# Attention of a two-layer kernel: the value products cut into two halves of 256 queries, in slots 1 and 3, and the key projection moved from slot 1 to slot 2

## The chip, the cores and the metric

The kernel runs on one core of one Trainium2 chip. The metric is the device time of one execution in microseconds, the median of several runs. Engines are named as in the profile: PE (TensorE, matrix products), PEld (its weight loads, which overlap PE), DVE (VectorE), ACT (ScalarE), POOL (GpSimd) and SP (SyncE, which issues most transfers).

## What is computed

Two layers act on `x` (8 batches of 512 tokens, 256 wide) and a context of the same shape. The first has a gated linear attention (mLSTM) and an MLP; the second has a softmax attention with 16 heads of 64 and a mixture of eight experts. All data is f32. The change touches only the softmax attention:

```python
q = query @ W_Query + B_Query          # W_*: 256 x 1024
k = key @ W_Key + B_Key                # key = value = the context
v = value @ W_Value + B_Value
q = q.reshape(B, Lq, H, D)             # H = 16, D = 64
k = k.reshape(B, Lk, H, D)
v = v.reshape(B, Lk, H, D)
scores = jnp.einsum('bqhd,bkhd->bhqk', q, k) / D ** 0.5
probs = jax.nn.softmax(scores, axis=-1)
out = jnp.einsum('bhqk,bkhd->bqhd', probs, v).reshape(B, Lq, H * D)
return out @ W_Output + B_Output
```

## The kernel before

`attention` works through U = 64 units `u`: 8 batches times 8 pairs of heads. The two heads of a pair fill the 128 partitions (64 each). A unit has NBL = 8 blocks `j`: head `j // 4`, 128 queries each. Each engine runs a program written out by hand, and all of them walk through the same loop: for every unit, eight slots `j` from 0 to 7. The text calls the score product of block j S(j) and the turn (the transposing product) of block j T(j).

The steps of a block are:

- S(j), in slot j, on PE (`score`, L917): two products of 128x512 in fp32r, into one of two banks of PSUM (`j % 2`). S(j) waits until the exponential of block j-2 has read that bank.
- the row maximum on DVE (L1052), the exponential with its row sum on ACT (L1009), the reciprocal of the sum on DVE (L1057), the scaling of the 128x512 block on POOL (L1030).
- T(j) on PE (`turn`, L928): four transposes of 128x128, in slot j+2 (T(6) and T(7) fall into slots 0 and 1 of the next unit). It waits for POOL.
- the copy of the turned block into `PT` on DVE (`keep`, L1064), for j = 4 and 5 on ACT (L1022).

Around these blocks PE does the rest of the unit's neighbours. `project` (L896, four passes of 512 columns) makes the queries of unit u+1 in slot 0 and its keys in slot 1. `weigh_values` (L938) makes the value products of unit u-1 in slot 2. `project_values` (L905) makes the values of u+1 in slot 4, and `output` (L948) the output products of u-1 in slots 5 and 6:

```python
if j < 2 and there(u + 1):
    project(u + 1, j)
if j == 2 and there(u - 1):
    weigh_values(u - 1)
```

In `weigh_values`, each head's V is the stationary operand with 64 columns. Head 0 goes to the left half of the array (PSUM partitions 0 to 63) and head 1 to the right half, so the products of the two heads run side by side. All other products of this loop use the array as 128 x 128. One product of f32 stands in the trace as two instructions: the eight products of `weigh_values` are 16 records. The first waits for all eight turned copies of the unit, for V, and for the output additions of the unit before (`x`); the last raises `pv`. On ACT `heads_out` (L995) then copies bank O_BANK to `oT`, before the exponential of slot 4, and `output` reads `oT`. ACT's `keys` (L985, in slot 1) and DVE's `keys` (L1046, in slot 2) write the two parts of `k_own`, and SP then copies them into `k2` with four transfers (L879), which S(0) of the next unit waits for. `add_out` (L1071) on DVE adds the output products to x in slot 7.

Of the kernel before, what the change touches and what calls it, by code (L numbers as in the profile page):

```python
# [21 lines left out]
P = 128  # L22
B, S, D = 8, 512, 256
N = B * S
TPB = S // P
# [5 lines left out]
AH, AD = 16, 64  # L31
# [794 lines left out]
def attention(nc, c, x_all, xnT_all, ctxT_all, first, Wq, Wk, Wv, Wo):  # L826
# [3 lines left out]
    with ExitStack() as ctx:  # L830
# [36 lines left out]
        with nc.Block() as block:  # L867
# [15 lines left out]
            def _(pe):  # L883
# [47 lines left out]

                def weigh_values(u):
                    wait_turned_copies(pe, u, NBL)
                    pe.wait_ge(s["V"], u + 1)
                    wait_count(pe, s["x"], 2 * u)
                    for t in range(TPB):
                        for h in range(2):
                            ins = pe.matmul(ps[AD * h:AD * h + AD, O_BANK, :], V[:, u % 2, t, AD * h:AD * h + AD],  # L938
                                            PT[:, u % 2, h, t, :], start=t == 0, stop=t == TPB - 1)
                    ins.then_inc(s["pv"], 1)  # L940

# [13 lines left out]
                for u in range(U + 1):  # L955
                    for j in range(NBL):
# [4 lines left out]
                        if j < 2 and there(u - 1):  # L961
                            turn(u - 1, NBL - 2 + j)
                        if j < 2 and there(u + 1):
                            project(u + 1, j)
                        if j == 2 and there(u - 1):
                            weigh_values(u - 1)
                        if j == 4 and there(u + 1):
# [5 lines left out]
            def _(act):  # L973
# [28 lines left out]
                for u in range(U + 1):  # L1002
                    for j in range(NBL):
                        if j == 4 and there(u - 1):
                            heads_out(u - 1)
                        if there(u):
                            act.wait_ge(s["nmax"], NBL * u + j + 1)
                            wait_count(act, s["t_ps"], NBL * u + j - 3)
                            act.activation(Pr[:, j % 4, :], ps[:, S_BANK + j % 2, :], ACT.Exp,  # L1009
                                           bias=nmax[:, j % 4:j % 4 + 1], accum_out=rsum[:, j % 4:j % 4 + 1]  # L1010
                                           ).then_inc(s["exp"], 1)
                        if there(u + 1):
                            if j == 0:
                                queries(u + 1)
                            if j == 1:
                                keys(u + 1)
# [17 lines left out]
            def _(dve):  # L1034
# [48 lines left out]
                for u in range(U + 1):  # L1083
                    for j in range(NBL):
# [8 lines left out]
                        if there(u + 1):  # L1093
                            if j == 1:
                                queries(u + 1)
                            if j == 2:
                                keys(u + 1)
# [635 lines left out]
```

## Time and profile before

| | before |
|---|---|
| median of 3 runs | 1862.72 us (1861.0 to 1865.55) |
| the profiled execution, own time | 1861.19 us |
| its span | 1859.5 us |
| PE busy in the span | 1683.3 us (91%) |
| DVE, ACT, POOL busy | 1192.0, 842.8, 619.9 us |
| mean granted clock of TensorE | 0.943 of full speed |

The span is the stretch from the first to the last record of the profiled execution; its own time is 1.7 us longer. An engine's busy time counts the stretches in which at least one of its instructions stands in the records. The ends of PE's records are modelled, so distances between starts say more about PE than the durations do. The attention lies roughly between 460 and 1640 us.

### The profile page before, as it was taken

The numbers are of one execution on the slowest core, as the hardware profiler recorded it, in microseconds if no ns is written. First come the engines' busy times: TensorE is split into PE (matmuls) and PEld (weight loads), VectorE is DVE, ScalarE is ACT, GpSimd is POOL, SyncE is SP. The second block draws the span as 40 slices with busy tenths as digits, with TensorE's granted clock in tenths as the row PEclk, the third lists the DMA queues.
The fourth block names the chain that finished last, engine by engine and source line by source line (L and its number), as shares of the span: only waits on it lengthen the run. The fifth ranks groups of instructions, "written<-read, shape, count | busy, mean of one in ns | idle before, by whom it ended". The sixth has DMA issues, their size and how long they took to land. (4 is left out here: it accounts for less than half of the span.)

```text
span 1859.5 us, 26060 instructions
## 1 busy us (share of the span) xinstructions
PE 1683.3 (91%) x8890; PEld 1152.6 (62%) x8890; DVE 1192.0 (64%) x2642; ACT 842.8 (45%) x1870; POOL 619.9 (33%) x746
## 2 busy tenths in 40 slices
PE   6469999996999999999999999999999999873584
PEld 4357777764666666666666666666666666572352
DVE  6444454432777777777777777777777777667761
ACT  3324443431555555555555555555555555421110
POOL 2154444430333232333333233232323232210375
PEclk9669999997999999999999999999999999955797
DMA  7100000003323222232323223232322223144144
GB/s 258 21 22 13 12 12 1 1 0 105 69 46 69 53 61 64 51 69 46 69 48 67 56 58 68 46 69 46 68 51 64 58 57 69 23 146 132 44 85 57
DMA packets 66657, 109.46 MB, mean 59 GB/s; under 512 B 16088, under 2 KB 48096, under 8 KB 66528
## 3 DMA queue, kind: packets, MB, share of 16 engines
q1 hardware_dynamic: 60384, 99.29, 21.8%
q0 software_dynamic: 6144, 8.52, 2.8%
q8 instruction: 72, 1.18, 0.3%
q14 instruction: 57, 0.47, 0.1%
HBM read 27.84 MB, written 12.85 MB: 22 GB/s over the span
## 5 line engine op out<-in xcount | busy, mean ns | idle before, releaser
L1030 POOL TENSOR_SCALAR at_Pr<-at_Pr,at_rinv 128x512 f32<-128x512 f32 x512 | 354.1, 692 | 826.7 <-DVE at_rinv L1057 826.7
L1009 ACT ACTIVATE at_Pr<-at_ps,at_nmax 128x512 f32<-128x512 f32 x512 | 352.0, 687 | 522.7 <-DVE at_nmax L1052 521.1
L1052 DVE TENSOR_REDUCE at_nmax<-at_ps 128x1 f32<-128x512 f32 x512 | 350.9, 685 | 139.0 <-PE at_ps L917 128.0
L917 PE MATMUL at_ps<-at_k,at_q 128*128 128x512 f32 x1024 | 420.8, 492 | 9.7 <-DMA at_k<-at_k_own 8.0
L928 PE MATMUL at_ps<-k_ident,at_Pr 128*128 128x128 f32 x2048 | 310.5, 274 | 4.0 <-POOL at_Pr L1030 4.0
L928 PEld LDWEIGHTS at_ps<-k_ident,at_Pr 128*128 128x128 f32 x2048 | 249.5, 140 | 93.2 <-POOL at_Pr L1030 32.8
L1064 DVE COPY at_PT<-at_ps 128x512 f32<-128x512 f32 x384 | 261.3, 681 | 0.0
L917 PEld LDWEIGHTS at_ps<-at_k,at_q 128*128 128x128 f32 x1024 | 174.6, 191 | 129.6 <-issue 120.1
L938 PE MATMUL at_ps<-at_PT,at_V 128*64 128x512 f32 x1024 | 233.8, 598 | 0.9 <-DVE at_PT L1064 0.9
L1057 DVE RECIPROCAL at_rinv<-at_rsum 128x1 f32<-128x1 f32 x512 | 83.3, 163 | 174.5 <-ACT at_Pr L1009 172.5
L938 PEld LDWEIGHTS at_ps<-at_PT,at_V 128*64 128x64 f32 x1024 | 67.7, 136 | 121.5 <-issue 120.3
L948 PE MATMUL at_ps<-at_wo,at_oT 128*128 128x256 f32 x512 | 131.6, 380 | 0.8 <-ACT at_oT L995 0.8
L458 PE MATMUL mm_ps<-mx_w,mm_hT 128*128 128x256 f32 x512 | 120.2, 381 | 0.0
L448 PE MATMUL mm_ps<-m_xnT,mx_w 128*128 128x512 f32 x256 | 111.2, 592 | 1.3 <-ACT m_xnT L601 1.3
L905 PE MATMUL at_ps<-at_w_rest,m_ctxT 128*128 128x128 f32 x896 | 109.2, 275 | 0.0
L896 PE MATMUL at_ps<-m_xnT,at_w_rest 128*128 128x512 f32 x224 | 107.1, 601 | 0.0
L896 PE MATMUL at_ps<-m_ctxT,at_w_rest 128*128 128x512 f32 x224 | 105.5, 593 | 0.0
L905 PEld LDWEIGHTS at_ps<-at_w_rest,m_ctxT 128*128 128x128 f32 x896 | 104.5, 192 | 0.0
L458 PEld LDWEIGHTS mm_ps<-mx_w,mm_hT 128*128 128x128 f32 x512 | 94.2, 190 | 15.5 <-issue 3.8
L1039 DVE SCALAR_TENSOR_TENSOR at_q<-at_ps,m_b_all,at_q 64x512 fp32r<-64x512 f32 x128 | 96.0, 750 | 8.4 <-ACT at_q L978 5.4
L1009 ACT ACTIVATION_READ_ACCUMULATOR at_Pr<-at_ps,at_nmax 128x1 f32 x512 | 98.7, 193 | 0.0
L948 PEld LDWEIGHTS at_ps<-at_wo,at_oT 128*128 128x128 f32 x512 | 87.4, 190 | 8.3 <-ACT at_oT L995 1.7
(237 smaller groups left out, 2030.5 us busy)
## 6 DMA issues: line engine op xcount, KB each, us to landing
at_k<-at_k_own SPq DMA_DIRECT2D x256, 256.0 KB, 4.1
k_x<-in_x SPq DMA_DIRECT2D x8, 512.0 KB, 7.8
mg_ctx<-in_ctx SPq DMA_DIRECT2D x8, 512.0 KB, 8.0
mx_ctxn<-in_ctx SPq DMA_DIRECT2D x8, 512.0 KB, 3.9
rows<-lo_xn SPq DMA_DIRECT2D x8, 512.0 KB, 3.0
out<-k_x SPq DMA_DIRECT2D x1, 4096.0 KB, 14.6
r_w<-in_L_ffn_w SPq DMA_DIRECT2D x16, 256.0 KB, 5.6
mx_w<-in_L_ffn_w SPq DMA_DIRECT2D x2, 1024.0 KB, 9.8
```

What stands on the lines that cost most here:

```text
L448: ins = pe.matmul(ps[:, H_BANK + f % 4, :], w1_s[:, k, P * f:P * f + P], xnT_all[:, k, b * S:b * S + S], start=k == 0, stop=k == DC - 1)
L458: ins = pe.matmul(ps[:, Y_BANK + t // 2, D * (t % 2):D * (t % 2) + D], hT[:, f, P * t:P * t + P], w2_s[:, f, :], start=f == 0, stop=f == F ...
L896: ins = pe.matmul(ps[:, A_BANK + k, :], weights(k, d, hp), src[:, d, b * S:b * S + S], start=d == 0, stop=d == DC - 1)
L905: ins = pe.matmul(ps[:, A_BANK, P * t:P * t + P], ctxT_all[:, d, b * S + P * t:b * S + P * t + P], weights(2, d, hp), start=d == 0, stop=d ...
L917: ins = pe.matmul(ps[:, S_BANK + j % 2, :], q2[:, u % 2, h, q:q + P], k2[:, u % 2, h, part, :], start=part == 0, stop=part == 1)
L928: ins = pe.transpose(ps[:, T_BANK + j % 2, P * t:P * t + P], Pr[:, j % 4, P * t:P * t + P], c["ident"][:, :])
L938: ins = pe.matmul(ps[AD * h:AD * h + AD, O_BANK, :], V[:, u % 2, t, AD * h:AD * h + AD], PT[:, u % 2, h, t, :], start=t == 0, stop=t == TP ...
L948: ins = pe.matmul(ps[:, Y_BANK - half, D * (t % 2):D * (t % 2) + D], oT[:, P * t:P * t + P], wo_s[:, u % HP, :], start=True, stop=True)
L1009: act.activation(Pr[:, j % 4, :], ps[:, S_BANK + j % 2, :], ACT.Exp, bias=nmax[:, j % 4:j % 4 + 1], accum_out=rsum[:, j % 4:j % 4 + 1]).th ...
L1030: pool.tensor_scalar(Pr[:, n % 4, :], Pr[:, n % 4, :], rinv[:, n % 4:n % 4 + 1], 1.0, ALU.mult, ALU.mult).then_inc(s["pn"], 1)
L1052: dve.tensor_reduce(nmax[:, j % 4:j % 4 + 1], ps[:, S_BANK + j % 2, :], AX.X, ALU.max, negate=True).then_inc(s["nmax"], 1)
L1064: dve.tensor_copy(PT[:, u % 2, j // TPB, :, q:q + P], ps[:, T_BANK + j % 2, :].rearrange("p (t q) -> p t q", t=TPB)).then_inc(s["pt_v"], 1)
```

## The change

`weigh_values` takes a half: the first makes queries 0 to 255 of both heads, in slot 1, the second queries 256 to 511, in slot 3. The weights V are the same for both. Within `PT` a block j of either head covers queries `128 * (j % 4)` onwards; the first half waits for the copies of blocks 0 to 5 and the second for all eight. `pv` is raised after the second. The key projection of the next unit moves from slot 1 to slot 2, and ACT's `keys` from slot 1 to slot 2 and DVE's from slot 2 to slot 3 with it. On ACT, `heads_out` goes behind the exponential of slot 4.

```diff
--- before.py
+++ after.py
@@ -929,15 +929,20 @@
                                            c["ident"][:, :])
                     ins.then_inc(s["t_ps"], 1)
 
-                def weigh_values(u):
-                    wait_turned_copies(pe, u, NBL)
-                    pe.wait_ge(s["V"], u + 1)
-                    wait_count(pe, s["x"], 2 * u)
+                def weigh_values(u, half):
+                    if half == 0:
+                        wait_turned_copies(pe, u, NBL - 2)
+                        pe.wait_ge(s["V"], u + 1)
+                        wait_count(pe, s["x"], 2 * u)
+                    else:
+                        wait_turned_copies(pe, u, NBL)
+                    at = slice(2 * P * half, 2 * P * half + 2 * P)
                     for t in range(TPB):
                         for h in range(2):
-                            ins = pe.matmul(ps[AD * h:AD * h + AD, O_BANK, :], V[:, u % 2, t, AD * h:AD * h + AD],
-                                            PT[:, u % 2, h, t, :], start=t == 0, stop=t == TPB - 1)
-                    ins.then_inc(s["pv"], 1)
+                            ins = pe.matmul(ps[AD * h:AD * h + AD, O_BANK, at], V[:, u % 2, t, AD * h:AD * h + AD],
+                                            PT[:, u % 2, h, t, at], start=t == 0, stop=t == TPB - 1)
+                    if half:
+                        ins.then_inc(s["pv"], 1)
 
                 def output(u, half):
                     if half == 0:
@@ -960,10 +965,10 @@
                                 turn(u, j - 2)
                         if j < 2 and there(u - 1):
                             turn(u - 1, NBL - 2 + j)
-                        if j < 2 and there(u + 1):
-                            project(u + 1, j)
-                        if j == 2 and there(u - 1):
-                            weigh_values(u - 1)
+                        if j in (0, 2) and there(u + 1):
+                            project(u + 1, j // 2)
+                        if j in (1, 3) and there(u - 1):
+                            weigh_values(u - 1, j // 2)
                         if j == 4 and there(u + 1):
                             project_values(u + 1)
                         if j in (5, 6) and there(u - 1):
@@ -1001,18 +1006,18 @@
                 values(0)
                 for u in range(U + 1):
                     for j in range(NBL):
-                        if j == 4 and there(u - 1):
-                            heads_out(u - 1)
                         if there(u):
                             act.wait_ge(s["nmax"], NBL * u + j + 1)
                             wait_count(act, s["t_ps"], NBL * u + j - 3)
                             act.activation(Pr[:, j % 4, :], ps[:, S_BANK + j % 2, :], ACT.Exp,
                                            bias=nmax[:, j % 4:j % 4 + 1], accum_out=rsum[:, j % 4:j % 4 + 1]
                                            ).then_inc(s["exp"], 1)
+                        if j == 4 and there(u - 1):
+                            heads_out(u - 1)
                         if there(u + 1):
                             if j == 0:
                                 queries(u + 1)
-                            if j == 1:
+                            if j == 2:
                                 keys(u + 1)
                             if j == 5:
                                 values(u + 1)
@@ -1093,7 +1098,7 @@
                         if there(u + 1):
                             if j == 1:
                                 queries(u + 1)
-                            if j == 2:
+                            if j == 3:
                                 keys(u + 1)
                         if j == 7:
                             if there(u):
```

On PE, from the score product of slot 1 to the projection of the values in slot 4, the program of before has (L917 is a score product, L928 a turn, L896 the key projection, L938 the value products, L905 the projection of the values; one row for what stands together):

```order
L917 MATMUL at_ps<-at_k,at_q 128x512 x2
L928 MATMUL at_ps<-k_ident,at_Pr 128x128 x4
L896 MATMUL at_ps<-m_ctxT,at_w_rest 128x512 x2
L917 MATMUL at_ps<-at_k,at_q 128x512 x2
L928 MATMUL at_ps<-k_ident,at_Pr 128x128 x4
L938 MATMUL at_ps<-at_PT,at_V 64x512 x8
L917 MATMUL at_ps<-at_k,at_q 128x512 x2
L928 MATMUL at_ps<-k_ident,at_Pr 128x128 x4
L917 MATMUL at_ps<-at_k,at_q 128x512 x2
L928 MATMUL at_ps<-k_ident,at_Pr 128x128 x4
L905 MATMUL at_ps<-at_w_rest,m_ctxT 128x128 x8
```

And the changed program over the same slots (L942 are the value products now):

```order
L917 MATMUL at_ps<-at_k,at_q 128x512 x2
L928 MATMUL at_ps<-k_ident,at_Pr 128x128 x4
L942 MATMUL at_ps<-at_PT,at_V 64x256 x8
L917 MATMUL at_ps<-at_k,at_q 128x512 x2
L928 MATMUL at_ps<-k_ident,at_Pr 128x128 x4
L896 MATMUL at_ps<-m_ctxT,at_w_rest 128x512 x2
L917 MATMUL at_ps<-at_k,at_q 128x512 x2
L928 MATMUL at_ps<-k_ident,at_Pr 128x128 x4
L942 MATMUL at_ps<-at_PT,at_V 64x256 x8
L917 MATMUL at_ps<-at_k,at_q 128x512 x2
L928 MATMUL at_ps<-k_ident,at_Pr 128x128 x4
L905 MATMUL at_ps<-at_w_rest,m_ctxT 128x128 x8
```

The one group of eight value products with 512 columns became two groups of eight with 256 columns, each between a turn and a score product, and the key projection stands between the groups.

On ACT, from the exponential of slot 1 on (L1009 exponentials, L985 keys, L995 `heads_out`, L990 values, L1022 a turned copy), before:

```order
L1009 ACTIVATE at_Pr,at_rsum<-at_ps,at_nmax 128x512
L985 ACTIVATE at_k_own<-at_ps,m_b_all 128x512
L1009 ACTIVATE at_Pr,at_rsum<-at_ps,at_nmax 128x512 x2
L995 ACTIVATE at_oT<-at_ps,m_b_all 128x512
L1009 ACTIVATE at_Pr,at_rsum<-at_ps,at_nmax 128x512 x2
L990 COPY at_V<-at_ps 128x512
```

and in the changed program (the same operations are L1012, L990, L1000, L995 and L1027):

```order
L1012 ACTIVATE at_Pr,at_rsum<-at_ps,at_nmax 128x512 x2
L990 ACTIVATE at_k_own<-at_ps,m_b_all 128x512
L1012 ACTIVATE at_Pr,at_rsum<-at_ps,at_nmax 128x512 x2
L1000 ACTIVATE at_oT<-at_ps,m_b_all 128x512
L1012 ACTIVATE at_Pr,at_rsum<-at_ps,at_nmax 128x512
L995 COPY at_V<-at_ps 128x512
```

The keys went one exponential later, and `heads_out` too.

## Rows read from the trace of the kernel before

**Rows 1.** The page: busy time of each engine over the whole span.
```profile
PE 1683.3 (91%) x8890; PEld 1152.6 (62%) x8890; DVE 1192.0 (64%) x2642; ACT 842.8 (45%) x1870; POOL 619.9 (33%) x746
```

**Rows 2.** Busy time by stretch; columns in the first row; steady part of the attention.
```profile
core 0: us, PE busy (x) PEld busy (x) DVE busy (x) ACT busy (x) POOL busy (x), PEclk, DMA share, GB/s
...
1000.00:1300.00 300.00, 300.00 (x1582) 197.55 (x1582) 221.69 (x447) 167.01 (x382) 91.45 (x133) 1.00 0.26 57
```

**Rows 3.** Timeline of PE, one unit: start us, us, engine, line, operation, tiles, count.
```profile
1007.87 0.60 PE L928 MATMUL at_ps<-k_ident,at_Pr 128*128 128x128 f32 x4
1008.40 3.65 PE L938 MATMUL at_ps<-at_PT,at_V 128*64 128x512 f32 x16
1011.98 0.74 PE L917 MATMUL at_ps<-at_k,at_q 128*128 128x512 f32 x2
1012.56 0.60 PE L928 MATMUL at_ps<-k_ident,at_Pr 128*128 128x128 f32 x4
1012.91 0.71 PE L917 MATMUL at_ps<-at_k,at_q 128*128 128x512 f32 x2
1013.47 0.60 PE L928 MATMUL at_ps<-k_ident,at_Pr 128*128 128x128 f32 x4
...
1016.15 0.60 PE L928 MATMUL at_ps<-k_ident,at_Pr 128*128 128x128 f32 x4
1016.59 1.03 PE L948 MATMUL at_ps<-at_wo,at_oT 128*128 128x256 f32 x4
...
1017.92 0.60 PE L928 MATMUL at_ps<-k_ident,at_Pr 128*128 128x128 f32 x4
...
1019.70 0.60 PE L928 MATMUL at_ps<-k_ident,at_Pr 128*128 128x128 f32 x4
...
1020.73 0.66 PE L928 MATMUL at_ps<-k_ident,at_Pr 128*128 128x128 f32 x4
1021.23 1.88 PE L896 MATMUL at_ps<-m_xnT,m_w_first 128*128 128x512 f32 x4
...
1023.41 0.60 PE L928 MATMUL at_ps<-k_ident,at_Pr 128*128 128x128 f32 x4
1023.85 1.88 PE L896 MATMUL at_ps<-m_ctxT,m_w_first 128*128 128x512 f32 x4
...
1026.03 0.60 PE L928 MATMUL at_ps<-k_ident,at_Pr 128*128 128x128 f32 x4
```

**Rows 4.** Timeline of the weight loads (PEld); in brackets, idle time before.
```profile
1008.40 0.20 PEld L938 LDWEIGHTS at_ps<-at_PT,at_V 128*64 128x64 f32 x4 [0.17 <-issue]
1008.88 0.14 PEld L938 LDWEIGHTS at_ps<-at_PT,at_V 128*64 128x64 f32 x2 [0.29 <-issue]
...
1011.03 0.14 PEld L938 LDWEIGHTS at_ps<-at_PT,at_V 128*64 128x64 f32 x2 [0.28 <-issue]
1011.98 0.30 PEld L917 LDWEIGHTS at_ps<-at_k,at_q 128*128 128x128 f32 x2 [0.81 <-issue]
...
1020.73 0.42 PEld L928 LDWEIGHTS at_ps<-k_ident,at_Pr 128*128 128x128 f32 x4 [0.40 <-POOL at_Pr L1030]
```

**Rows 5.** Timeline of the other engines and of SP's queue, same unit.
```profile
1007.92 0.19 ACT L1009 ACTIVATION_READ_ACCUMULATOR at_Pr<-at_ps,at_nmax 128x1 f32 x1
...
1011.22 3.75 SPq L879 DMA_DIRECT2D at_k<-at_k_own  x4
...
1012.76 0.69 DVE L1052 TENSOR_REDUCE at_nmax<-at_ps 128x1 f32<-128x512 f32 x1 [1.55 <-PE at_ps L917]
...
1014.16 0.68 ACT L995 ACTIVATE at_oT<-at_ps,m_b_all 128x512 f32<-128x512 f32 x1
...
1019.99 0.69 POOL L1030 TENSOR_SCALAR at_Pr<-at_Pr,at_rinv 128x512 f32<-128x512 f32 x1 [1.08 <-DVE at_rinv L1057]
```

**Rows 6.** Costliest groups, shapes apart: count, busy us, mean ns of one.
```profile
L948 PE MATMUL at_ps<-at_wo,at_oT 128*128 128x256 f32 x512 | 131.6, 380 | 0.8 <-ACT at_oT L995 0.8
```

## Prediction

> **What bounds the kernel now.** I read the busy times first. PE stands at 91% of the span and the next engine at 64% [rows 1]. In the steady part of the attention PE is busy for all of 300 us, at a granted clock of 1.00 (the 2.4 GHz level), while DVE has 222 us and the others less [rows 2]. But the ends of PE's records are modelled, so "100% busy" could hide waits. So I went to the timeline of PE and measured the distances between the starts of turns; one stands in each slot [rows 3]. The reader is to see that almost every distance is what the products in it need:
>
> - T(1) to T(2), with nothing but a score product between: 1013.47 - 1012.56 = 0.91 us.
> - T(7) to T(0), with the key projection between: 1026.03 - 1023.41 = 2.62 us.
> - T(0) to T(1), with the value products between: 1012.56 - 1007.87 = 4.69 us.
> - T(5) to T(6): 1020.73 - 1019.70 = 1.03 us, 0.12 more than the 0.91 above.
>
> The length of one 512-column pass comes from the weight loads: from 1008.88 to 1011.03 are five passes of a pair of heads, 2.15 / 5 = 0.43 us [rows 4]. The four passes of a projection are then 1.72 us, and 2.62 - 1.72 = 0.90 us is left for a score product and a turn: the same as the 0.91 of the slot that has nothing else. So the slots with a projection hold no wait at all. The unit repeats every 1026.03 - 1007.87 = 18.16 us, and 64 of these are 1162 us, most of the stretch of the attention.
>
> Two things in the unit are not PE's own work. One is the 0.12 us at T(6), which waits for POOL: its scaling ends at 1020.68 [rows 5] and the weight load starts at 1020.73, after 0.40 us of idle time that mostly lies beside the score product [rows 4]. The other is in the value products. Their eight pairs are 8 x 0.43 = 3.44 us, a score and a turn 0.90, together 4.34, and the distance is 4.69: **0.35 us more**. The weight loads show where it lies. At the entrance, the first load stands 0.17 us after the turn's loads, and the next pair's load at 1008.88 puts the start of the first pair at 1008.45, 0.15 us after the end of T(0)'s pass work (1007.87 + 0.43 = 1008.30). At the exit, the load for S(3) comes at 1011.98 after 0.81 us without a load, where 0.28 or 0.29 is the rule [rows 4]; that is the other 0.20. Nothing that S(3) waits for is open then: the exponential that frees its bank had ended at 1008.11 [rows 5]. The row maximum of the same block sat idle for 1.55 us waiting for PE [rows 5], so the other engines follow PE here and not the reverse.
>
> The page "TensorEngine Tiling (Array Packing)" of the Trainium skill, section on tiling modes, says that a change of tiling mode drains the engine. The value products are the only ones of the loop in the form 128*64, and the trace agrees as to place: both parts of the 0.35 us stand exactly where the form changes.
>
> **The change, part by part.**
>
> 1. *A second block of value products.* The form of the products now changes four times in a unit and not twice: turn to value products to score product, in slot 1 and again in slot 3. What one such visit costs the row above gives, 0.35 us. The bounds for the new one: nothing, if the excess goes by the columns and not by the visit; and the whole 0.35. A first pair and a last pair exist in each half as they do in the whole, so I take the upper end: +0.35 us per unit.
>
> 2. *256 columns instead of 512.* A unit has 16 pairs of passes of 256 columns for 8 of 512. The nearest rows are the output products, 256 columns with full weights: four records last 1.03 us and one 0.380 [rows 3, 6], so they follow each other by (1.03 - 0.38) / 3 = 0.217 us. The 16 pairs are 3.47 us for 3.44: +0.03 us. V is loaded twice as often. A pair's loads take 0.14 us [rows 4], less than 0.217, so they stay covered by the pair ahead; without that cover each would add up to 0.14 (a rival, below).
>
> 3. *The key projection in slot 2.* The same four passes, 1.72 us, between T(0) and T(1) now. On PE it costs nothing either way.
>
> 4. *What the moved steps may make late.* ACT's and DVE's parts of the keys come one slot later; the four transfers start about 2 us later in the unit. They took 3.75 us from 1011.22 on [rows 5] and are needed at S(0), which stands between T(5) at 1019.70 and T(6) at 1020.73: some 5 us were spare, 3 remain. `heads_out` now waits for the exponential of S(4). Before, it ended at 1014.16 + 0.68 = 1014.84, that is 2.86 us after the start of the score product that followed the value products (1011.98) [rows 3, 5]. After the change that product is S(4), with the exponential of that block again ahead of `heads_out`. The output products start 1016.59 - 1012.91 = 3.68 us after S(4) [rows 3], so `oT` is there 0.8 us early. Priced at nothing; the cover is the projection of the values between them.
>
> 5. *The wait of T(6).* Slots 4 to 7 keep their order on all engines but for `heads_out`, and the chain from S(6) to T(6) is the same. I leave its 0.12 us as it is, so the more even filling of the early slots wins nothing: there was no wait in them.
>
> **The sum.** From T(7) to T(2), before: 2.62 + 4.69 + 0.91 = 8.22 us. After: 0.90 + 8 x 0.217 + 0.35 = 2.99 for each half, and 2.62 for the keys: 8.60 us. That is +0.38 us per unit, times 64 units = +24.3 us. Against the profiled execution's own 1861.2 us this gives **1885.5 us**. (That execution lies 1.5 us below the median of the runs shown.) Outside the attention nothing changes.
>
> **Rivals.**
>
> *A. A pair of heads cannot be fed at 0.217 us.* Two loads and two products have to be started for each pair. Take the turns: four single loads and products in 0.60 us [rows 3], so 0.15 each if nothing is taken off for the end of the last. If two tiles needed 2 x 0.15 = 0.30 us per pair, each pair would be 0.083 longer, 16 x 0.083 = 1.33 us per unit, and the time 1861.2 + 64 x (0.38 + 1.33) = 1971 us. Against it: four loads of 64 columns stand within 0.20 us at 1008.40 [rows 4]. Chance 0.06. The same page of the Trainium skill, section on instruction overhead, gives some 60 cycles for each matmul; as an estimate from it, 16 more instructions per unit at 25 ns (60 cycles of 2.4 GHz) would be 0.4 us per unit and the sum 1911 us in place of 1885.5. The trace speaks against it: two output products of 256 columns take 0.434 us, one pass of 512 takes 0.43.
>
> *B. A new wait.* Turns T(0) and T(1), or the output products, meet POOL or ACT late, as T(6) does now. Two more waits of 0.12 us are 0.24 us per unit: 1861.2 + 64 x 0.62 = 1901 us, the upper end; larger ones lie above. Chance of lying above 1902 by this: 0.06.
>
> *C. Faster: the 0.35 us is a wait for another engine.* `weigh_values` now waits for all eight turned copies, and its first half will need only six, which are long done; if the engine waited at the entrance, and S(3) at the exit, for work of DVE or ACT, both waits go when the work is spread, and T(6) gains its 0.12 us as well. Then the unit changes by -0.35 - 0.12 + 0.03 = -0.44 us, and the time is 1833 us. It decides the matter if the load of the score product after the value products stands at its regular 0.2 to 0.3 us of idle time. Against it speak the exponential that was done 3.9 us before S(3)'s load, and the profile, which names no engine ("issue") for either idle time. Chance 0.05.
>
> *D. The excess goes by columns.* Each half pays half of 0.35, and only the 0.03 us of step 2 is left: 1863 us, no change. Chance 0.05.
>
> **How the numbers follow.** The forecast has 0.78; A and B together 0.12, all slower; C 0.05, faster; D 0.05, the same. A difference under 0.3% (5.6 us) can hardly be told from none by a measurement of this kernel. So faster 0.05, the same 0.05, slower 0.90. The range: below, only the entrance (0.15 us) is paid again, 1861.2 + 64 x 0.15 = 1871; above, the two new waits of B, 1902. C, D, A and what of B lies above are left out, under 2 in 10.
>
> **What would show it.** In the changed kernel's trace two blocks of value products of about 1.9 us each stand in a unit; T(7) to T(0) and T(1) to T(2) are each 2.99 us, T(0) to T(1) is 2.62 us, and a unit is 18.5 us. The weight loads of the score products in slots 2 and 4 come late, after 0.5 us or more without a load, and those within a block every 0.22 us. PE is still busy throughout at clock 1.00, and T(6) still waits for POOL. I am wrong in step 1 if a block's excess over its pairs is well under 0.35 us, in step 2 if the pairs follow each other at over 0.23 us, in steps 4 and 5 if turns or output products show idle time before them that names POOL, ACT or a transfer. A unit of less than 18.1 us overturns the whole reading.

## The result, and the profile after

| | before | after |
|---|---|---|
| median | 1861.86 us (4 runs, 1860.43 to 1865.55) | 1886.31 us (4 runs, 1880.68 to 1888.89) |
| ratio to before, 95% interval | | 1.0124 [1.0097, 1.0152] |
| the profiled execution, own time | 1861.19 us | 1880.68 us |
| its span | 1859.5 us | 1879.0 us |

The change makes the kernel 24.5 us slower by the medians; 1885.5 us had been forecast, with a range from 1871 to 1902. Busy times over the whole span, from the page of the changed kernel (before: [rows 1]):

```profile
PE 1704.6 (91%) x9914; PEld 1220.2 (65%) x9914; DVE 1199.2 (64%) x2642; ACT 843.2 (45%) x1870; POOL 620.0 (33%) x746
```

And the stretch from 1000 to 1300 us, in the columns of [rows 2]:

```profile
1000.00:1300.00 300.00, 299.87 (x1817) 211.27 (x1815) 219.05 (x439) 163.22 (x373) 89.64 (x130) 1.00 0.25 57
```

PE is still busy practically throughout at a granted clock of 1.00. Its weight loads went from 197.55 to 211.27 us in the stretch, because V is loaded twice as often, and DVE's busy time fell a little, from 221.69 to 219.05 us: the same work per unit, over longer units.

The timeline of PE over one unit, from T(6) to the next T(6), to be read beside [rows 3] (L942 are the value products, L953 the output products):

```profile
1011.48 0.66 PE L928 MATMUL at_ps<-k_ident,at_Pr 128*128 128x128 f32 x4
...
1014.16 0.60 PE L928 MATMUL at_ps<-k_ident,at_Pr 128*128 128x128 f32 x4
1014.69 1.95 PE L942 MATMUL at_ps<-at_PT,at_V 128*64 128x256 f32 x16
...
1017.14 0.60 PE L928 MATMUL at_ps<-k_ident,at_Pr 128*128 128x128 f32 x4
1017.57 1.88 PE L896 MATMUL at_ps<-m_ctxT,at_w_rest 128*128 128x512 f32 x4
...
1019.76 0.60 PE L928 MATMUL at_ps<-k_ident,at_Pr 128*128 128x128 f32 x4
1020.29 1.95 PE L942 MATMUL at_ps<-at_PT,at_V 128*64 128x256 f32 x16
...
1022.74 0.60 PE L928 MATMUL at_ps<-k_ident,at_Pr 128*128 128x128 f32 x4
...
1025.43 0.60 PE L928 MATMUL at_ps<-k_ident,at_Pr 128*128 128x128 f32 x4
1025.86 1.03 PE L953 MATMUL at_ps<-at_wo,at_oT 128*128 128x256 f32 x4
...
1028.97 0.60 PE L928 MATMUL at_ps<-k_ident,at_Pr 128*128 128x128 f32 x4
...
1030.01 0.66 PE L928 MATMUL at_ps<-k_ident,at_Pr 128*128 128x128 f32 x4
```

Two blocks of value products of 1.95 us stand where one of 3.65 us stood. The distances of the turns are 1017.14 - 1014.16 = 2.98 us around the first, 2.62 us around the key projection, 1022.74 - 1019.76 = 2.98 us around the second. Their sum, 8.58 us, was 8.22 before. T(2) to T(3) is 2.69 us and T(5) to T(6) 1.04 us, nearly as before. A unit lasts 1030.01 - 1011.48 = 18.53 us and lasted 18.16. Between 700 and 1500 us, the distance around a half is 2.97 or 2.98 us in every unit. The weight loads at the borders of a block:

```profile
1014.69 1.49 PEld L942 LDWEIGHTS at_ps<-at_PT,at_V 128*64 128x64 f32 x16 [0.17 <-issue]
1016.57 0.30 PEld L917 LDWEIGHTS at_ps<-at_k,at_q 128*128 128x128 f32 x2 [0.39 <-issue]
```

At the entrance there is the same idle time of 0.17 us as in [rows 4]. At the exit it is 0.39 us. The 16 loads of a block (8 pairs) are drawn together into one row of 1.49 us, since only short gaps are left between them (0.217 - 0.14, some 0.08 us); before, 0.28 or 0.29 us lay idle between two pairs.

The first and last score product of the attention tell the rest. Group of the score products in the trace of the kernel before, then of the changed one (shortest, median and longest in ns, then the first and last start in us):

```profile
L917 PE MATMUL at_ps<-at_k,at_q x1024: 392/474/1415, 457.9 to 1617.3; 128*128 128x512 f32 x171
```

```profile
L917 PE MATMUL at_ps<-at_k,at_q x1024: 391/467/1382, 453.7 to 1638.1; 128*128 128x512 f32 x171
```

From the first to the last score product are 1617.3 - 457.9 = 1159.4 us before and 1638.1 - 453.7 = 1184.4 us after: the attention lost 25.0 us. That the two spans differ by 19.5 us only has its reason outside the change: in this execution the attention began 4.2 us earlier, and what follows it was 1.3 us shorter. The medians, 24.5 us apart, don't depend on that.

### The profile page after: what moved, and what is told of

The parts are those of the page before. It is cut to its first block and busy times, and to the rows that moved or that the text cites. A ratio compares the mean times of both kernels' runs of the same rounds, so it can differ in the third digit from the quotient of the medians.

```text
span 1879.0 us, 28172 instructions
## 1 busy us (share of the span) xinstructions
PE 1704.6 (91%) x9914; PEld 1220.2 (65%) x9914; DVE 1199.2 (64%) x2642; ACT 843.2 (45%) x1870; POOL 620.0 (33%) x746
## 5 line engine op out<-in xcount | busy, mean ns | idle before, releaser
L1012 ACT ACTIVATE at_Pr<-at_ps,at_nmax 128x512 f32<-128x512 f32 x512 | 352.0, 687 | 545.7 <-DVE at_nmax L1057 544.1
L917 PE MATMUL at_ps<-at_k,at_q 128*128 128x512 f32 x1024 | 422.4, 494 | 10.7 <-DMA at_k<-at_k_own 10.2
L928 PE MATMUL at_ps<-k_ident,at_Pr 128*128 128x128 f32 x2048 | 310.7, 274 | 3.2 <-POOL at_Pr L1035 3.2
L928 PEld LDWEIGHTS at_ps<-k_ident,at_Pr 128*128 128x128 f32 x2048 | 250.0, 141 | 90.9 <-POOL at_Pr L1035 29.3
L917 PEld LDWEIGHTS at_ps<-at_k,at_q 128*128 128x128 f32 x1024 | 174.4, 190 | 128.7 <-issue 117.9
L942 PE MATMUL at_ps<-at_PT,at_V 128*64 128x256 f32 x2048 | 249.0, 385 | 0.0
L942 PEld LDWEIGHTS at_ps<-at_PT,at_V 128*64 128x64 f32 x2048 | 135.7, 136 | 76.8 <-issue 21.1
L953 PE MATMUL at_ps<-at_wo,at_oT 128*128 128x256 f32 x512 | 131.8, 380 | 1.6 <-ACT at_oT L1000 1.6
L905 PE MATMUL at_ps<-at_w_rest,m_ctxT 128*128 128x128 f32 x896 | 109.2, 275 | 0.0
L896 PE MATMUL at_ps<-m_xnT,at_w_rest 128*128 128x512 f32 x224 | 108.0, 606 | 0.0
L896 PE MATMUL at_ps<-m_ctxT,at_w_rest 128*128 128x512 f32 x224 | 105.4, 593 | 0.0
L905 PEld LDWEIGHTS at_ps<-at_w_rest,m_ctxT 128*128 128x128 f32 x896 | 104.5, 192 | 0.0
L1012 ACT ACTIVATION_READ_ACCUMULATOR at_Pr<-at_ps,at_nmax 128x1 f32 x512 | 98.6, 193 | 0.0
L953 PEld LDWEIGHTS at_ps<-at_wo,at_oT 128*128 128x128 f32 x512 | 87.4, 190 | 8.9 <-ACT at_oT L1000 2.3
```

The costliest lines, as they stand in the source:

```text
L896: ins = pe.matmul(ps[:, A_BANK + k, :], weights(k, d, hp), src[:, d, b * S:b * S + S], start=d == 0, stop=d == DC - 1)
L905: ins = pe.matmul(ps[:, A_BANK, P * t:P * t + P], ctxT_all[:, d, b * S + P * t:b * S + P * t + P], weights(2, d, hp), start=d == 0, stop=d ...
L917: ins = pe.matmul(ps[:, S_BANK + j % 2, :], q2[:, u % 2, h, q:q + P], k2[:, u % 2, h, part, :], start=part == 0, stop=part == 1)
L928: ins = pe.transpose(ps[:, T_BANK + j % 2, P * t:P * t + P], Pr[:, j % 4, P * t:P * t + P], c["ident"][:, :])
L942: ins = pe.matmul(ps[AD * h:AD * h + AD, O_BANK, at], V[:, u % 2, t, AD * h:AD * h + AD], PT[:, u % 2, h, t, at], start=t == 0, stop=t == ...
L953: ins = pe.matmul(ps[:, Y_BANK - half, D * (t % 2):D * (t % 2) + D], oT[:, P * t:P * t + P], wo_s[:, u % HP, :], start=True, stop=True)
```

## The experiments

The theory of the prediction (**the visit**) says that each group of value products between products of another form costs 0.35 us of PE, whatever the number of columns, and that nothing else in the change costs more than the 0.03 us of the narrower products. Its rivals are that the cost goes by columns or by the cut itself, that it is a wait for another engine, and that the moved steps have a price. All times below stand beside runs of the kernel before on the same chip.

### One visit, 256 columns

The kernel before, with the two halves one after the other in slot 2.

```diff
-                    for t in range(TPB):
-                        for h in range(2):
+                    for half in range(2):
+                        at = slice(2 * P * half, 2 * P * half + 2 * P)
+                        for t in range(TPB):
+                            for h in range(2):
...
+                                                PT[:, u % 2, h, t, at], start=t == 0, stop=t == TPB - 1)
```

> The two halves of 256 queries stand together in slot 2, nothing else is moved. Theory of the visit (each change of the products' form costs its share of 0.35 us, however many columns stand between): one visit per unit as before, only 16 pairs of 256 columns for 8 of 512, +0.03 us per unit, +2 us in all; the distance of the turns around the value products is 4.72 us. Theory of the cut (the excess comes with a group of products of its own accumulation, or with the narrower products): +0.35 us and more per unit, +24 us, distance 5.0 to 5.1 us.

1863.66 us against 1863.06, ratio 1.0005 [0.9992, 1.0018]. Timeline of PE, T(0) to T(1):

```profile
1009.56 0.60 PE L928 MATMUL at_ps<-k_ident,at_Pr 128*128 128x128 f32 x4
1010.08 3.67 PE L940 MATMUL at_ps<-at_PT,at_V 128*64 128x256 f32 x32
...
1014.26 0.60 PE L928 MATMUL at_ps<-k_ident,at_Pr 128*128 128x128 f32 x4
```

The distance is 4.70 us for 4.69: sixteen pairs of 256 columns are 0.01 us longer than eight of 512. (Between 700 and 1500 us the medians of this distance are 4.70 and 4.68.) The cut by itself costs next to nothing.

### Two visits, 512 columns

The products keep their width and are cut by key tile, in slots 2 and 3; the keys stay in slot 1.

```diff
-                    for t in range(TPB):
+                    for t in (2 * part, 2 * part + 1):
...
-                        if j == 2 and there(u - 1):
-                            weigh_values(u - 1)
+                        if j in (2, 3) and there(u - 1):
+                            weigh_values(u - 1, j - 2)
```

> The value products keep their 512 columns and are cut by key tiles: tiles 0 and 1 in slot 2, tiles 2 and 3 in slot 3; the key projection stays where it was. Theory of the visit: two visits per unit, +0.35 us per unit, +22 us; the two distances around the value products are 0.90 + 1.72 + 0.35 = 2.97 us each. Theory of the columns (the excess is shared out over the columns, or comes with the cut into 256): 4.69 + 0.91 us for the two slots as before, no change in the time.

1885.58 us against 1863.06, ratio 1.0132 [1.011, 1.0154]: +22.5 us, the loss of the change without its narrow products and without its moved keys. PE from T(0) to T(1) to T(2):

```profile
1019.37 0.60 PE L928 MATMUL at_ps<-k_ident,at_Pr 128*128 128x128 f32 x4
1019.90 1.94 PE L939 MATMUL at_ps<-at_PT,at_V 128*64 128x512 f32 x8
...
1022.34 0.60 PE L928 MATMUL at_ps<-k_ident,at_Pr 128*128 128x128 f32 x4
...
1025.30 0.60 PE L928 MATMUL at_ps<-k_ident,at_Pr 128*128 128x128 f32 x4
```

2.97 and 2.96 us, together 5.93, where the two slots took 4.69 + 0.91 = 5.60 us.

### Four visits

The same cut into four groups of two pairs each, two of them between a score product and its turn.

```diff
+                        if j in (3, 4) and there(u - 1):
+                            weigh_values(u - 1, 2 * j - 5)
...
-                        if j == 2 and there(u - 1):
-                            weigh_values(u - 1)
+                        if j in (2, 3) and there(u - 1):
+                            weigh_values(u - 1, 2 * j - 4)
```

> 512 columns, cut by key tile into four groups of two pairs: after the turn of slot 2, between score product and turn of slot 3, after that turn, and between score product and turn of slot 4. Theory of the visit: four visits, three more than before, 3 x 0.35 us per unit, +67 us to about 1929 us. If the cost of a second visit is right but does not add up: less than 45 us.

1923.02 us against 1861.84, ratio 1.0319 [1.0302, 1.0335]: +61.2 us for three more visits in 64 units, 0.32 us each. PE:

```profile
1017.43 0.60 PE L928 MATMUL at_ps<-k_ident,at_Pr 128*128 128x128 f32 x4
1017.96 1.08 PE L938 MATMUL at_ps<-at_PT,at_V 128*64 128x512 f32 x4
...
1019.63 1.08 PE L938 MATMUL at_ps<-at_PT,at_V 128*64 128x512 f32 x4
1020.64 0.66 PE L928 MATMUL at_ps<-k_ident,at_Pr 128*128 128x128 f32 x4
...
1023.91 0.66 PE L928 MATMUL at_ps<-k_ident,at_Pr 128*128 128x128 f32 x4
```

T(0) to T(1) is 3.21 us, of which 0.90 are score and turn and 4 x 0.43 the pairs, so 0.59 us for two visits. T(1) to T(2), with the other two groups, is 3.27 us, so 0.65 for two. The costs add up, at slightly less than 0.35 us each.

### No other form in the loop

The kernel before with weights of 128 columns and the turned block of the first head alone. The second head's value products are left out; PE has the same number of 512-column passes, since those of two heads had run side by side.

```diff
-                        for h in range(2):
-                            ins = pe.matmul(ps[AD * h:AD * h + AD, O_BANK, :], V[:, u % 2, t, AD * h:AD * h + AD],
-                                            PT[:, u % 2, h, t, :], start=t == 0, stop=t == TPB - 1)
+                        ins = pe.matmul(ps[:, O_BANK, :], V[:, u % 2, t, :], PT[:, u % 2, 0, t, :],
+                                        start=t == 0, stop=t == TPB - 1)
```

> The kernel before, with all 128 columns of V as weights and the turned block of the first head alone as the moving side: the value products of the second head are left out, PE has the same 8 passes of 512 columns, and no product of the loop has another form than 128*128. Theory of the visit: the 0.35 us go, -22 us to about 1839 us, the distance around the value products is 4.34 us and the score product's weight load behind them comes after the regular 0.2 to 0.3 us of idle time. Theory that the excess is a wait for another engine or belongs to any group of eight: 4.69 us stays, no change.

1840.92 us against 1863.06, ratio 0.9886 [0.9867, 0.9905]: -22.1 us. PE from T(0) to T(1), and then the first weight load of S(3):

```profile
1013.16 0.60 PE L928 MATMUL at_ps<-k_ident,at_Pr 128*128 128x128 f32 x4
1013.60 3.60 PE L937 MATMUL at_ps<-at_PT,at_V 128*128 128x512 f32 x8
...
1017.50 0.60 PE L928 MATMUL at_ps<-k_ident,at_Pr 128*128 128x128 f32 x4
```

```profile
1016.61 0.19 PEld L917 LDWEIGHTS at_ps<-at_k,at_q 128*128 128x128 f32 x1 [0.24 <-issue]
```

The distance is 4.34 us, which is what the pairs, the score product and the turn need, and the load of S(3) comes after 0.24 us of idle time like any other. The 0.35 us are gone with the form.

The changed kernel with the same omission:

```diff
-                        for h in range(2):
-                            ins = pe.matmul(ps[AD * h:AD * h + AD, O_BANK, at], V[:, u % 2, t, AD * h:AD * h + AD],
-                                            PT[:, u % 2, h, t, at], start=t == 0, stop=t == TPB - 1)
+                        ins = pe.matmul(ps[:, O_BANK, at], V[:, u % 2, t, :], PT[:, u % 2, 0, t, at],
+                                        start=t == 0, stop=t == TPB - 1)
```

> The changed kernel with the same omission (second head's value products left out, weights of 128 columns): halves of 256 columns in slots 1 and 3, one form throughout. Theory of the visit: nothing is left of the two excesses, distances of 2.62 to 2.66 us in all three slots, time within 4 us of the whole version in the same form, about 1840 us. Theory that the early slots wait for ACT, DVE or POOL in the new order: this kernel stays slower than that one by a good part of 24 us.

1846.24 us, ratio 0.9920 [0.9899, 0.9940]. The turns stand 2.63, 2.62 and 2.63 us apart, without any excess. So of the 24 us between the two orders 5.3 are left by the medians, a little over the 4 us allowed. In the two traces the attention, from the first to the last score product, takes 1594.9 - 455.5 = 1139.4 us in the version with whole products and 1600.9 - 453.6 = 1147.3 in the one with halves, 7.9 more. The distances account for 1.3 of them (7.88 us for 2.62 + 4.34 + 0.90 = 7.86, times 64). The list of waits has nearly all of the rest: score products waited for the transfers of the keys once in the first (8.3 us, at the start), and 15 times, 14.8 us in all, in the second (us in total, times, longest):

```profile
PE at_ps L917 <- DMA at_k<-at_k_own: 14.8, 15, 7.7
```

So what is left between the two orders is no cost of the value products on PE but the later keys, of which the next section speaks.

### The moved steps

Two kernels were to show that the moves are free; neither did, and both say something about the change. In the first the keys go to slot 3, and the value products stay whole in slot 2.

```diff
-                        if j < 2 and there(u + 1):
-                            project(u + 1, j)
+                        if j in (0, 3) and there(u + 1):
+                            project(u + 1, j // 3)
...
-                            if j == 1:
+                            if j == 3:
                                 keys(u + 1)
...
-                            if j == 2:
+                            if j == 4:
                                 keys(u + 1)
```

> The value products whole in slot 2 as before; the key projection goes to slot 3 on PE, ACT's keys to slot 3 and DVE's to slot 4, and heads_out behind the exponential of slot 4. What the moves alone cost. Theory of the visit: nothing, within 4 us of the kernel before (the slot of 0.91 us becomes one of 2.62, slot 1 shrinks to 0.91). Theory that the moves make a wait (keys late, output late): up to +24 us, with idle time of PE before the score product of slot 0 or the output products.

2034.1 us against 1861.84, ratio 1.0925 [1.0897, 1.0953]: +172 us, against the expectation of the visit's theory. The list of waits (us in total, times, longest) has the following row, where the kernel before has one such wait, of 8.0 us at the start. So it names 148.5 of the 172 us; what makes up the rest was not followed.

```profile
PE at_ps L917 <- DMA at_k<-at_k_own: 156.5, 64, 8.1
```

And the timeline of one unit has DVE's part of the keys and the S(0) that needs them:

```profile
1016.45 0.74 DVE L1046 SCALAR_TENSOR_TENSOR at_k_own<-at_ps,m_b_all,at_k_own 128x512 fp32r<-128x512 f32 x1
...
1024.15 0.71 PE L917 MATMUL at_ps<-at_k,at_q 128*128 128x512 f32 x2 [2.27 <-DMA at_k<-at_k_own]
```

The keys are ready at 1017.19 and S(0) starts at 1024.15: 6.96 us for four transfers to be issued and to land. In the kernel before, DVE's keys ended at 1011.14 and S(0) stood at 1020.05, 8.91 us later:

```profile
1010.40 0.74 DVE L1046 SCALAR_TENSOR_TENSOR at_k_own<-at_ps,m_b_all,at_k_own 128x512 fp32r<-128x512 f32 x1
...
1020.05 0.72 PE L917 MATMUL at_ps<-at_k,at_q 128*128 128x512 f32 x2
```

The second kernel has exactly the moves of the change, and the value products whole in slot 3. (Shown are the rows of PE; those of ACT and DVE are moved as in the change. The first kernel also has `heads_out` behind the exponential of slot 4.)

```diff
-                        if j < 2 and there(u + 1):
-                            project(u + 1, j)
-                        if j == 2 and there(u - 1):
+                        if j in (0, 2) and there(u + 1):
+                            project(u + 1, j // 2)
+                        if j == 3 and there(u - 1):
                             weigh_values(u - 1)
```

> All that the change moves, without its cut: the key projection in slot 2, ACT's keys in slot 2, DVE's in slot 3, heads_out behind the exponential of slot 4, and the value products whole, with 512 columns, in slot 3. Theory of the visit, with the loss of the moves-alone kernel put down to the key transfers being one slot later there than in the change: one visit as before, keys early enough (over 9 us from DVE's keys to S(0), where 7 were needed), no change, within 4 us of the kernel before. Theory that the moves of the change have a price of their own (output late, turns late): up to some +20 us, and the visit would be cheaper than 0.35 us.

1950.48 us against 1865.33, ratio 1.0476 [1.0455, 1.0496]: +85.2 us, with only two waits for a transfer of the keys, both among the first units (9.6 us in all, 7.9 of them at the start). All engines around slot 1:

```profile
1021.40 1.29 DVE L1071 TENSOR_TENSOR k_x<-at_ps,k_x 128x512 f32<-128x512 f32 x2
...
1022.60 0.68 DVE L1052 TENSOR_REDUCE at_nmax<-at_ps 128x1 f32<-128x512 f32 x1
...
1023.32 0.60 PE L928 MATMUL at_ps<-k_ident,at_Pr 128*128 128x128 f32 x4
...
1024.46 0.69 POOL L1030 TENSOR_SCALAR at_Pr<-at_Pr,at_rinv 128x512 f32<-128x512 f32 x1 [2.12 <-DVE at_rinv L1057]
...
1025.21 0.66 PE L928 MATMUL at_ps<-k_ident,at_Pr 128*128 128x128 f32 x4 [0.32 <-POOL at_Pr L1030]
```

Slot 1 holds only a score product and a turn now, 0.9 us of PE's work. Block 0 comes late there: DVE adds two outputs to x first (1021.40 to 1022.69), then takes the row maximum, and POOL's scaling ends at 1025.15. T(0) waits for it. T(7) to T(0) is 1025.21 - 1023.32 = 1.89 us where 0.91 would do, T(0) to T(1) 2.93 (T(1), at 1028.14, waits for POOL as well, whose scaling of block 1 ends at 1028.09), and T(1) to T(2) 4.74. The three are 9.56 us against 8.22, and 64 x 1.34 = 86 us is the whole loss. So whatever stands in slot 1 does two jobs, its own and the cover for block 0. The change takes the keys out and puts the first half in, and the changed kernel's trace shows that this covers block 0:

```profile
1015.32 0.69 POOL L1035 TENSOR_SCALAR at_Pr<-at_Pr,at_rinv 128x512 f32<-128x512 f32 x1 [2.12 <-DVE at_rinv L1062]
```

The scaling ends at 1016.01, 1.13 us before T(0) at 1017.14. That is why the move of the keys costs PE nothing there. (In the first kernel slot 1 was empty too, but T(7) to T(0) is 0.90 us in its trace: there S(0) comes so late that DVE's additions are over before block 0 needs DVE.)

To see how far the changed kernel is from the wait for the keys, one step was made later in it: DVE's keys in slot 4.

```diff
-                            if j == 3:
+                            if j == 4:
                                 keys(u + 1)
```

> The changed kernel with one step later: DVE's part of the keys in slot 4 and not in slot 3. In the changed kernel it ends 7.4 us before S(0); in the moves-alone kernel S(0) was released 6.96 us after it. DVE's keys would end some 3.1 us later, so if a fixed time of 7 us stands between them and S(0), S(0) waits 2.5 to 2.7 us in each unit and the kernel takes about 2050 us. If the transfers had the 3 us to spare that the prediction gave them, less than 10 us would be lost.

2059.49 us, ratio 1.1049 [1.1028, 1.107]; 173 us over the changed kernel's median, 2.7 us per unit. DVE's keys and S(0):

```profile
1006.17 0.74 DVE L1051 SCALAR_TENSOR_TENSOR at_k_own<-at_ps,m_b_all,at_k_own 128x512 fp32r<-128x512 f32 x1
...
1014.00 0.70 PE L917 MATMUL at_ps<-at_k,at_q 128*128 128x512 f32 x2 [2.40 <-DMA at_k<-at_k_own]
```

From 1006.91 to 1014.00 are 7.09 us. In the changed kernel the same two stand as follows, with SP's issue, `heads_out` and T(6)'s wait between them:

```profile
1021.17 0.74 DVE L1051 SCALAR_TENSOR_TENSOR at_k_own<-at_ps,m_b_all,at_k_own 128x512 fp32r<-128x512 f32 x1
...
1021.98 3.13 SPq L879 DMA_DIRECT2D at_k<-at_k_own  x4
...
1024.34 0.68 ACT L1000 ACTIVATE at_oT<-at_ps,m_b_all 128x512 f32<-128x512 f32 x1
...
1029.33 0.72 PE L917 MATMUL at_ps<-at_k,at_q 128*128 128x512 f32 x2
...
1030.01 0.42 PEld L928 LDWEIGHTS at_ps<-k_ident,at_Pr 128*128 128x128 f32 x4 [0.40 <-POOL at_Pr L1035]
```

From 1021.91 to 1029.33 are 7.42 us: S(0) finds its keys with 0.3 to 0.5 us to spare, where the kernel before had some 1.9. Three times in this execution S(0) did wait for them, 10.2 us in all, of which 8.0 are the one wait at the start. The halves in one form have still less to spare: there the interval is 7.04 us in the median between 700 and 1500 us, which is why S(0) waited 15 times.

The page of the kernel before already had a figure that speaks of the landing (KB of one transfer, then the median from issue to landing in us):

```profile
at_k<-at_k_own SPq DMA_DIRECT2D x256, 256.0 KB, 4.1
```

An estimate from it: the four issues took 3.75 us [rows 5], the last of them 0.60 if it is like the median one in that trace, and its landing follows 4.1 us after its start. That is 3.75 - 0.60 + 4.1 = 7.25 us from the first issue, and would have left S(0) of the kernel before about 1.6 us to spare and not 5. Measured are 7.0 to 7.1 us from the end of DVE's keys.

### The wait of T(6)

The kernel before, with one row moved in slot 0 of PE:

```diff
+                        if j == 0 and there(u + 1):
+                            project(u + 1, j)
                         if j < 2 and there(u - 1):
                             turn(u - 1, NBL - 2 + j)
-                        if j < 2 and there(u + 1):
+                        if j == 1 and there(u + 1):
                             project(u + 1, j)
```

> The kernel before with one row moved on PE: in slot 0 the query projection stands ahead of the turn T(6), which waits for POOL. My reading: T(6)'s wait of 0.12 us is covered by 1.72 us of projection, -0.12 us per unit, -8 us to about 1854 us. Rival: the turn's later start delays the copy of block 6 and with it the value products, which wait for all eight copies: no gain or a loss of some us.

1852.04 us against 1861.84, ratio 0.9933 [0.9915, 0.9951]. It was measured again:

> The kernel before with the query projection ahead of T(6), again, in five rounds: -8 to -10 us against the kernel before (ratio 0.993 to 0.996), distance T(5) to T(6) of 2.62 us with the projection in it, T(6) to T(7) 0.91 us. If the first measurement was luck: a ratio within 0.3% of 1.

1848.83 us against 1865.33, ratio 0.9919 [0.9903, 0.9936]: 16.5 us less, where the first time it was 9.8 and 8 to 10 were expected. This kernel beats both. PE from T(5) over T(6) to T(7):

```profile
1013.21 0.60 PE L928 MATMUL at_ps<-k_ident,at_Pr 128*128 128x128 f32 x4
...
1014.12 1.88 PE L896 MATMUL at_ps<-m_xnT,m_w_first 128*128 128x512 f32 x4
1015.83 0.60 PE L928 MATMUL at_ps<-k_ident,at_Pr 128*128 128x128 f32 x4
...
1016.75 0.60 PE L928 MATMUL at_ps<-k_ident,at_Pr 128*128 128x128 f32 x4
```

T(5) to T(6), now with the projection in it, is 2.62 us and T(6) to T(7) 0.92, together 3.54; before, they were 1.03 + 2.68 = 3.71 us [rows 3]. The gain is 0.17 us per unit and 11 us in all, which lies between the two differences of the medians; from the first to the last score product the trace has 1147.5 us for 1159.4, 11.9 less. I had counted 0.12: the 2.68 behind the waiting turn was 0.06 too long as well.

The same row moved in the changed kernel:

> The changed kernel with the same row moved in slot 0 (query projection ahead of T(6)). Its first half waits for six copies only, so nothing can be late: -0.12 us per unit, -8 us against the changed kernel, to about 1878 us. Rival: the wait for POOL moves on to T(7), no gain.

1874.51 us, ratio to the kernel before 1.0061 [1.0044, 1.0079]: 11.8 us under the changed kernel's median, which was measured on another occasion, and more than the 8 expected, as with the kernel before. The two effects stand side by side.

A last candidate had in addition the value products between S(3) and T(1):

```diff
+                        if j == 3 and there(u - 1):
+                            weigh_values(u - 1)
...
-                        if j == 2 and there(u - 1):
-                            weigh_values(u - 1)
```

> A candidate to beat both kernels: the query projection ahead of T(6), and the value products, whole and with 512 columns, between the score product and the turn of slot 3 and no longer between T(0) and S(3). The kernel with four visits had two groups inside the distance T(0) to T(1), 3.21 us for 0.90 and four pairs of 0.43: 0.59 us for two visits, one behind a turn and one behind a score product, so 0.30 each. Theory of the visit: still one visit, 0.30 to 0.35 us, T(0) to T(1) 4.6 to 4.7 us, within 4 us of the kernel with the queries ahead alone (about 1850 us). If the visit's price falls on weight loads that a score product covers better than a turn does, up to 0.1 us per unit more is won, about 1844 us.

1856.45 us against 1864.82, ratio 0.9958 [0.9943, 0.9973]: faster than before, but not than with the queries ahead alone. In its timeline the distance with the value products in it, T(0) to T(1), is 4.75 us, not 4.69, and the light one behind it, T(1) to T(2), 0.97 instead of 0.91. The place behind a score product is no cheaper; it costs 0.12 us per unit more, 7.7 us in 64 units. By the medians this kernel lies 4.4 and 7.6 us above the two measurements of the one with the queries ahead alone.

## Why the prediction was right, point by point

**The bound.** PE bound the loop and still does; the distances between turns were the right measure, since the busy time says 100% before and after and can't tell the two kernels apart.

**Step 1, the second visit: right.** 0.35 us had been taken, the upper bound. The changed kernel shows 2.98 - 0.90 - 8 x 0.217 = 0.34 us per half. The two-visit kernel shows the loss without the narrow products, the four-visit kernel shows that it adds up (0.32 us each), and the kernel in one form shows that it vanishes with the form. Rival C, a wait for another engine, and rival D, a cost by columns, both fall with these three. Rival B, a new wait of the turns or the output products, is not there either: in the changed kernel's list of waits PE waits for POOL ahead of turns 3.2 us in all, for 4.0 before, and for `oT` ahead of the output products 1.6 us for 0.8. What the runs don't separate is the change of form from the running of two products side by side, as the full-form kernels dropped both; the drain at a change of mode of which the Trainium skill speaks ("TensorEngine Tiling (Array Packing)", section on tiling modes) fits the late load at the exit, and that page gives no price. A detail was off: the idle time ahead of the load at the exit was to be 0.5 us or more and is 0.39, since the last load of a block stands only one narrow pair ahead of its end. It is late all the same: the gap between narrow pairs is some 0.08 us.

**Step 2, the narrow products: right.** +0.03 us had been forecast and 0.01 to 0.02 were seen in the kernel with both halves together, and rival A has no trace: the pairs follow each other at 0.217 us or less. The overhead of about 60 cycles for each matmul, of which the Trainium skill speaks ("TensorEngine Tiling (Array Packing)", section on instruction overhead), does not show with 16 more of them. That section's example, a product of one column that takes as long as one of 60, reads as a floor for short products rather than as an addition to long ones; no run here tests the floor.

**Step 3, the keys in slot 2: right, but not for the reason given.** "On PE it costs nothing either way" holds for PE's own work alone. Taken out of slot 1 without a replacement, the projection costs 1.34 us per unit, 1.29 of them ahead of T(0) and T(1), because it had covered the late block 0. The prediction ought to have named this cover: it had looked for waits only where the kernel before had one.

**Step 4, what becomes late: the result right, the margin wrong.** The price was nothing and is nearly that. But the 3 us that were to remain for the keys are 0.3 to 0.5. The row of SP with 3.75 us [rows 5] had been read as if it lasted until the keys had landed, but it shows the issues alone; the kernel before had 1.9 us to spare and not 5. How long the keys take shows where S(0) waits for them, 7.0 us after DVE's keys, and could have been estimated from the 4.1 us to landing. That the move still cost only 2.2 us in the whole execution (10.2 us of waits for 8.0) was luck. The transfers also start only 1.5 us later against S(0) and not 2 (7.35 us ahead of it for 8.83). `oT` was there in time as worked out: `heads_out` ends at 1025.02 and the output products start at 1025.86, 0.84 us later.

**Step 5, the wait of T(6): right in that it stays** (1.04 us from T(5) to T(6)), a third too small in what it is worth: 0.17 us and not 0.12.

**The sum.** +0.38 us per unit had been forecast; the distances gave 8.58 - 8.22 = 0.36, and the first to the last score product 25.0 us for 24.3; 64 x 0.36 = 23.0, and 2.2 are the waits for the keys. That the median came within 1 us of the forecast is more than either can vouch for: the runs of the changed kernel lie 8 us apart.

## What to carry to other kernels

Where an engine is busy throughout, moving its work about wins nothing but the waits that can be pointed at; measure them as distances between the starts of one repeating instruction and set them against the same distance in a slot without the suspected cost. A group of products in another array form has a price per visit, so such products belong together, and splitting them for the sake of evenness pays it again. Before taking a step out of a slot, ask what late arrival it covers there, and measure a transfer's margin from the write of its source to the first use, not by the row of its issue.

## What the runs showed of the hardware

- Going from products in the form 128*128 to pairs of 128*64 that run side by side, and back, cost 0.30 to 0.35 us per visit at the 2.4 GHz level. With one visit per unit, 0.15 of the 0.35 lies at the entrance and 0.20 at the exit, where the next weight load starts only when the block is over.
- Sixteen pairs of 256 columns took as long as eight of 512 within 0.02 us, and weights of 64 columns loaded for both tiles every 0.217 us stayed covered.
- Four transfers of 256 KB between two places on the chip, issued one after the other by SP, took 7.0 to 7.1 us from the end of the instruction that wrote their source to the start of the one that waited for them, while the row of their issue shows 3.1 to 3.8 us. From issue to landing a single one took 4.1 us in the median.
